# A perceiver block on one core: in 43 of the search's 64 steps the fourth tile's second count is made by ScalarE

## The reference, cut to what matters

```python
# channel_map: [16, 1601, 2048], x: [16, 64, 2048]
k = 38                                   # floor(0.6 * 64), made even
_, topk_idx = top_k(moveaxis(channel_map, 1, 2), k)      # 38 largest of 1601, for each of 16*2048 rows
mask = zeros((16, 2048, 64)).at[b, l, topk_idx].set(1.0) # only indices below 64 leave a mark
...                                      # two gated convolutions over mask * layernorm(x)
x = x + xattn(layernorm(x), channel_map, ...)
x = x + attention(layernorm(x), wq, wk, wv, wo)
x = x + ffn_with_experts(layernorm(x), ...)
```

## Time and profile before

| | |
|---|---|
| three runs | 2256.2, 2256.2, 2254.48 us |
| span of the profiled execution, first to last instruction | 2253.2 us (its own time is not listed apart) |
| the search, to the last decision of count a (L609 of step 64) | 651.1 us |
| TensorE busy | 1967.7 us, 87% |
| VectorE busy | 1368.3 us, 61% |
| ScalarE busy | 1062.3 us, 47% |
| GpSimd busy | 1185.0 us, 53% |

### The profile page before, as it was taken

How to read it: one execution, slowest core, us unless ns; L and a number is a source line. 1 busy time by engine, 2 the same in 40 slices (tenths; PEclk the granted TensorE clock), 3 DMA queues, 4 the chain that set the end, 5 groups by cost and what they waited for, 6 DMA issues and landing times. The chain is left out here.

```text
span 2253.2 us, 38992 instructions
## 1 busy us (share of the span) xinstructions
PE 1967.7 (87%) x14912; PEld 1573.5 (70%) x14912; DVE 1368.3 (61%) x2085; ACT 1062.3 (47%) x2441; POOL 1185.0 (53%) x1093
## 2 busy tenths in 40 slices
PE   4778788777761738999999999999999999999999
PEld 4666566555650237788778888877778878888887
DVE  6999999999999988744444611244446325631111
ACT  7877788788855665432332422232223322422222
POOL 3555555555546604755554546565555445644554
PEclk9999999999995869999999999999999999999999
DMA  9999999999942025522235443222254445434443
GB/s 388 376 369 373 329 327 326 310 314 325 335 150 80 17 68 163 173 81 78 82 109 178 141 138 115 88 77 81 80 173 141 127 145 192 146 117 136 139 137 114
DMA packets 158393, 407.67 MB, mean 181 GB/s; under 512 B 15616, under 2 KB 44544, under 8 KB 156544
## 3 DMA queue, kind: packets, MB, share of 16 engines
q1 hardware_dynamic: 157920, 403.55, 52.5%
q0 software_dynamic: 288, 1.64, 0.2%
HBM read 379.96 MB, written 25.17 MB: 180 GB/s over the span
## 5 line engine op out<-in xcount | busy, mean ns | idle before, releaser
L1348 POOL TENSOR_TENSOR t<-t,t 128x512 fp32r<-128x512 f32 (+1 forms) x488 | 650.0, 1343 | 662.8 <-ACT t L1341 590.9
L1899 PE MATMUL ps<-t,t 128*128 128x512 f32 x1856 | 739.0, 398 | 11.8 <-POOL t L1348 6.3
L1901 PE MATMUL ps<-t,t 128*128 128x512 f32 x1856 | 724.9, 391 | 0.0
L1900 PE MATMUL ps<-t,t 128*128 128x512 f32 x1856 | 724.5, 390 | 0.0
L1341 ACT ACTIVATE t<-t 128x512 fp32r<-128x512 f32 (+1 forms) x488 | 296.4, 608 | 697.0 <-PE ps L1901 372.8
L728 PE MATMUL ps<-t,t 128*128 128x128 bf16 (+1 forms) x6656 | 450.4, 222 | 165.0 <-DVE t L444 152.0
L728 PEld LDWEIGHTS ps<-t,t 128*128 128x128 bf16 x6656 | 388.9, 100 | 263.2 <-DVE t L444 231.0
L444 DVE TENSOR_SCALAR t<-t,t 128x1601 bf16<-128x1601 f32 x512 | 521.7, 1053 | 6.1 <-PE ps L728 2.0
L658 ACT ACTIVATE t<-t,t 128x1601 bf16<-128x1601 f32 x256 | 417.0, 1629 | 112.7 <-POOL t L686 110.3
L1899 PEld LDWEIGHTS ps<-t,t 128*128 128x128 f32 x1856 | 349.0, 188 | 92.2 <-POOL t L1348 11.0
L1901 PEld LDWEIGHTS ps<-t,t 128*128 128x128 f32 x1856 | 349.2, 188 | 74.7
(11 more groups left out here) (231 smaller groups left out, 1724.0 us busy)
## 6 DMA issues: line engine op xcount, KB each, us to landing
t<-ctxT SPq DMA_DIRECT2D x256, 800.5 KB, 6.5
t<-wqkv SPq DMA_DIRECT2D x192, 256.0 KB, 3.3
t<-wo SPq DMA_DIRECT2D x128, 256.0 KB, 4.7
t<-wb SPq DMA_DIRECT2D x128, 256.0 KB, 3.4
t<-xT SPq DMA_DIRECT2D x48, 256.0 KB, 6.6
t<-x1d SPq DMA_DIRECT2D x32, 256.0 KB, 4.9
x2d<-t SPq DMA_DIRECT2D x32, 256.0 KB, 2.0
t<-x2d SPq DMA_DIRECT2D x8, 1024.0 KB, 7.2
```

The source lines that it names most:

```text
L1348: e.tensor_tensor(wlo[r][:, 0:nk, :], raw[r][:, 0:nk, :], wh[r][:, 0:nk, :].bitcast(F32), ALU.subtract).then_inc(w_lo, 1)
L1899: e.matmul(bank[:, :], wh[r][:, q, :], xl, start=(kt == 0), stop=False)
L1900: e.matmul(bank[:, :], wlo[r][:, q, :], xh, start=False, stop=False)
L1901: m = e.matmul(bank[:, :], wh[r][:, q, :], xh, start=False, stop=(c == NCH[p] - 1 and q == nk - 1))
```

## The change

ScalarE makes count b of a quad's fourth tile, as a sum of signs, in 43 quads: g = 1 to 23, the odd g from 25 to 55, and 56 to 59. Quad g's count b falls into step g+1, so these are steps 2 to 24, the even steps 26 to 56, and steps 57 to 60. VectorE makes seven masks there. GpSimd makes the negated bound (`bound_b_gpsimd`) and takes the decision (`decide_b_gpsimd`). The order of the masks becomes b and c by turns. Where the quad two steps back is one of the 43, one b mask stands ahead of the decision of count b, otherwise two. GpSimd copies the candidates of two tiles in one instruction. The flags of the first 15 batches get five more operations. Some semaphores are merged, and an unused column block of the constants is left out.

```diff
+def by_act(g):
+    return 1 <= g < NQ - 4 and not (25 <= g + 1 <= 56 and g % 2 == 0)
+def front(i):
+    return 1 if by_act(i - 2) else 2
 def masks_of(i):
-    return [(k, u) for k, u in ORDER if (1 <= i <= NQ if k == "b" else 2 <= i <= NQ + 1)]
+    b = [("b", u) for u in range(3 if by_act(i - 1) else 4)] if 1 <= i <= NQ else []
+    c = [("c", u) for u in range(4)] if 2 <= i <= NQ + 1 else []
+    out = b[:front(i)]
+    b = b[front(i):]
+    while b and c:
+        out += [c.pop(0), b.pop(0)]
+    return out + b + c
...
     def sign_scalar(e, i, u):
...
+        if u == 2 and by_act(i - 1):
+            e.wait_ge(b_signed, ACT_NO[i - 1] + 1)
...
+    def sign_b_scalar(e, g):
+        n = 4 * g + 3
+        e.wait_ge(b_bound, ACT_NO[g] + 1)
+        e.wait_ge(signed, 4 * g + 6)
+        e.activation(scr[:, :], ring[n % NR][:, :], ACT.Sign, bias=nTB[:, g:g + 1], scale=SHRINK,
+                     accum_out=cntB[:, g % 8:g % 8 + 1]).then_inc(b_signed, 1)
...
     def search_scalar(e):
...
                 if u == 0 and 2 <= i:
                     counts_scalar(e, i - 1, 3)
+                if u == 1 and by_act(i - 1):
+                    sign_b_scalar(e, i - 1)
...
     def search_vector(e):
...
-                for u in range(2):
+                for u in range(front(i)):
                     mask_vector(e, i, "b", u, vg[:, u, 1:2])
...
-                e.wait_ge(counts_out, slot_of(i - 1, 3) + 1)
-                e.tensor_scalar(insB[:, 4 * c:4 * c + 4], sums[:, 4 * c:4 * c + 4], HIGH * K, None, ALU.is_lt).then_inc(b_dec, 1)
+                n = 3 if by_act(c) else 4
+                e.wait_ge(counts_out, slot_of(i - 1, n - 1) + 1)
+                e.tensor_scalar(insB[:, 4 * c:4 * c + n], sums[:, 4 * c:4 * c + n], HIGH * K, None, ALU.is_lt).then_inc(b_dec, 1)
                 e.wait_ge(b_dec, c + 1)
+                if by_act(c):
+                    e.wait_ge(b3_dec, ACT_NO[c] + 1)
...
+    def bound_b_gpsimd(e, g):
+        b, t = tile_of(4 * g + 3)
+        e.wait_ge(a_set, g + 1)
+        e.tensor_scalar(nTB[:, g:g + 1], v8[:, b % 2, t, 1:2], TINY, -1.0, ALU.max, ALU.mult).then_inc(b_bound, 1)
+
+    def decide_b_gpsimd(e, g):
+        e.wait_ge(b_signed, ACT_NO[g] + 1)
+        e.tensor_scalar(insB[:, 4 * g + 3:4 * g + 4], cntB[:, g % 8:g % 8 + 1], 2.0 * K - CM - 1.0, None,
+                        ALU.is_lt).then_inc(b3_dec, 1)
...
     def search_gpsimd(e):
...
+        for i in range(NQ):
+            if by_act(i - 2):
+                decide_b_gpsimd(e, i - 2)
+            bounds_gpsimd(e, i, 0)
+            if by_act(i - 1):
+                bound_b_gpsimd(e, i - 1)
+            copy_gpsimd(e, 4 * i)
+            if i >= 6 and (i - 6) % 4 == 0:
+                fin_gpsimd(e, (i - 6) // 4)
+            bounds_gpsimd(e, i, 1)
+            copy_gpsimd(e, 4 * i + 2)
+            quad_gpsimd(e, i)
```

More of the change, by code:

```diff
@@ L145 @@
 NQ = B * NT // 4
-ORDER = [("b", 0), ("b", 1), ("c", 0), ("b", 2), ("c", 1), ("b", 3), ("c", 2), ("c", 3)]
-def masks_of(i):
-    return [(k, u) for k, u in ORDER if (1 <= i <= NQ if k == "b" else 2 <= i <= NQ + 1)]
+def by_act(g):
+    return 1 <= g < NQ - 4 and not (25 <= g + 1 <= 56 and g % 2 == 0)
+ACT_B = [g for g in range(NQ) if by_act(g)]
+ACT_NO = {g: k for k, g in enumerate(ACT_B)}
+def front(i):
+    return 1 if by_act(i - 2) else 2
+def masks_of(i):
+    b = [("b", u) for u in range(3 if by_act(i - 1) else 4)] if 1 <= i <= NQ else []
[5 more added lines that the diff above has]
+    return out + b + c
 MASK_NO = {}
@@ L169, in slot_first @@
 def slot_first(i, u):
-    return MASK_NO[(i, "b", u)] if i <= NQ else MASK_NO[(i, "c", u)]
+    return min(MASK_NO[(i, k, u)] for k in "bc" if (i, k, u) in MASK_NO)
 def slot_last(i, u):
-    return MASK_NO[(i, "c", u)] if i >= 2 else MASK_NO[(i, "b", u)]
-def b_of(n):
-    return MASK_NO[(n // 4 + 1, "b", n % 4)]
+    return max(MASK_NO[(i, k, u)] for k in "bc" if (i, k, u) in MASK_NO)
 def c_of(n):
@@ L225, in build @@
     RS = (CM * 4 + 31) // 32 * 32
-    ring = [at(64 * KB + i * RS, [CM]) for i in range(NR)]
+    couples = [at(64 * KB + 2 * i * RS, [2, RS // 4]) for i in range(NR // 2)]
+    ring = [couples[i // 2][:, i % 2, 0:CM] for i in range(NR)]
+    heads = [couples[i][:, :, 0:C] for i in range(NR // 2)]
     o = 64 * KB + NR * RS
@@ L316, in build @@
     w16 = sb([16])
+    nTB = sb([NQ])
+    cntB = sb([8])
     sc = sb([80])
@@ L409, in setup_vector @@
     def setup_vector(e):
+        e.memset(nTB[:, :], -1.0)
         e.memset(fl2[:, :], 0.0).then_inc(set_up, 1)
@@ L485, in flags_vector @@
         w, wu = lsq[:, r], lsq[:, r].bitcast(U32)
+        nb, f3, ins3 = nTB[:, 4 * b0:4 * b1], last_of_four(f), last_of_four(insB[:, r])
+        w3, wu3 = w[:, 0:4 * (b1 - b0)], wu[:, 0:4 * (b1 - b0)]
         e.wait_ge(ln0_sqsum, 2 * NT)
-        for s in range(NFL):
+        for s in range(NFL[k]):
             if k or s:
-                e.wait_ge(flag_step, NFL * k + s)
+                e.wait_ge(flag_step, NFL[0] * k + s)
             if s == 0:
@@ L505, in flags_vector @@
                 i = e.tensor_tensor(f, f, w, ALU.max)
+            if s == 8:
+                i = e.scalar_tensor_tensor(w3, nb, -TINY, ins3, ALU.is_ge, ALU.mult)
+            if s == 9:
+                i = e.tensor_tensor(f3, f3, w3, ALU.max)
+            if s == 10:
+                i = e.tensor_scalar(wu3, nb.bitcast(U32), 0x7FFFFF, None, ALU.bitwise_and)
+            if s == 11:
+                i = e.tensor_scalar(w3, wu3, float(0x7FFFFF), None, ALU.is_equal)
+            if s == 12:
+                i = e.tensor_tensor(f3, f3, w3, ALU.max)
             i.then_inc(flag_step, 1)
@@ L638, in search_vector @@
                 maxima(1, 0)
-            for k, (kind, u) in enumerate(masks_of(i)):
-                if kind == "b" and u < 2:
+            todo = masks_of(i)
+            first = front(i) if i <= NQ else 0
+            for k, (kind, u) in enumerate(todo):
+                if k < first:
                     continue
                 mask_vector(e, i, kind, u, vg[:, u, 1:2] if kind == "b" else vc[:, u, 0:1])
-                done += 1
-                if 2 <= i < NQ and done == 3:
+                if 2 <= i < NQ and k == 2:
                     maxima(i, 1)
-                if 1 <= i < NQ - 1 and done == (4 if i == 1 else 7):
+                if 1 <= i < NQ - 1 and k == len(todo) - (1 if i == 1 else 2):
                     maxima(i + 1, 0)
-                if first_steps and i <= NQ + 1 and done <= 7:
-                    end_batch([done - 1])
+                if first_steps and k - first < 5:
+                    end_batch([2 + k - first])
                 if k == 4:
@@ L704, in quad_gpsimd, with copy_gpsimd @@
         e.tensor_tensor(eqb[y][:, four, :], v8[:, y, four, 0:7], v8[:, y, four, 1:8], ALU.subtract).then_inc(tied, 1)
-    def search_gpsimd(e):
[L707 to L718, removed]
+    def bound_b_gpsimd(e, g):
[6 more added lines that the diff above has]
+                        ALU.is_lt).then_inc(b3_dec, 1)
+    def copy_gpsimd(e, n):
+        b, t = tile_of(n)
+        if b >= 2 and t == 0:
+            e.wait_ge(fin, NF * (b - 2) + 8)
+        landed(e, n)
+        landed(e, n + 1)
+        e.tensor_copy(cand[b % 2][:, t:t + 2, :], heads[n % NR // 2]).then_inc(cand_copied, 1)
+    def search_gpsimd(e):
+        for i in range(NQ):
[10 more added lines that the diff above has]
+            quad_gpsimd(e, i)
     def count_tensor(e, i, kind, u):
@@ L784, in search_tensor @@
                     ln0_tensor(e, i, todo.pop(0))
+            for u in todo:
+                ln0_tensor(e, i, u)
     flags_max, flags_read, flags_all, row_in, turn_rows = (sem("flags_max"), sem("flags_read"), sem("flags_all"),
                                                            sem("row_in"), sem("turn_rows"))
-    turn_pick, turn_last, picked = sem("turn_pick"), sem("turn_last"), sem("picked")
+    turn_pick, turn_last, row_stage = sem("turn_pick"), sem("turn_last"), sem("row_stage")
+    PICKED, LEFT_KNOWN, OPENED = 1, 2, 3
     d_row, d_first = sem("d_row"), sem("d_first")
-    opened, segment, calm = sem("opened"), sem("segment"), sem("calm")
-    any_in, any_sum, flags_pool = sem("any_in"), sem("any_sum"), sem("flags_pool")
+    segment, calm = sem("segment"), sem("calm")
+    any_sum, flags_pool = sem("any_sum"), sem("flags_pool")
     any_left = ps[4][:, 0:1]
@@ L811, in first_pick_vector @@
         flags_vector(e, 0, 0, B - 1)
-        e.wait_ge(flag_step, NFL)
-        e.wait_ge(d_rid, 16)
+        e.wait_ge(flag_step, NFL[0])
+        e.wait_ge(d_const, N_CONST + 16)
         do = in_turn(e, turn_pick)
@@ L909, in rows_vector @@
             e.sem_inc(flags_max, 1)
-        e.memset(sm[:, 12:13], 0.0).then_inc(opened, 1)
+        e.memset(sm[:, 12:13], 0.0).then_inc(row_stage, 1)
     def gather_gpsimd(e, k, signal):
         e.wait_ge(masked, c_of(G_TILE[k]) + 1)
-        e.wait_ge(cand_copied, G_TILE[k] + 1)
```

(1 more changed line is left out.)

33 lines of the change are left out of this document (17 added, 16 removed).

## The result

The change makes the kernel slower, by a quarter of a per cent. Twenty runs gave a median of 2260.0 us (2254.6 to 2263.4) against 2254.4 us for twenty of the kernel before (2250.1 to 2259.9). The ratio is 1.0025, with a 95% interval of 1.0018 to 1.0032. I had forecast 2243.0 and a range up to 2254, a gain of 13.2 us where the medians show a loss of 5.6. The profiled execution has a span of 2260.4 us, 7.2 more than before.

A forecast was written before the change was run, and what follows sets the result against it. VectorE's order, mostly masks, was taken to bound the search, with ScalarE and the DMA close behind. Terms -1.7 - 13.8 + 1.2 + 1.1 = -13.2 us took the median from 2256.2 to 2243.0, range 2234 to 2254.

The forecast's parts named there:

- ScalarE's chain: ScalarE's distances from start to start in a step with the fifth sign: 9.64 us, or 9.97 with a square.
- A: Steps 2 to 24, 23 changed steps: 226.35 us before, forecast 224.7, a gain of 1.7 us.
- The rival in which ScalarE isn't the bound: Signs follow each other at 1.61 us, not 1.81; the DMA then sets steps 2 to 24; total 2229 us; 7%.
- The rival in which the DMA decides A: Steps 2 to 24: queues give only 364 GB/s, 9.97 us a step; total 2247.7 us; 12%.
- The bound's time: GpSimd's bound that sign 2 waits for: early by 0.5 us in ordinary steps, late by 0.6 with L472.
- B: Steps 26 to 56, 16 changed steps: VectorE stays the bound, 15.4 us go, 1.6 charged back, gain 13.8.
- The rival "B gives nothing": Steps 26 to 56: VectorE waits for ScalarE's fourth sign in each changed step; total 2255.8 us, no difference; 10%.
- C: Steps 57 to 60, 4 changed steps: 38.46 us before, forecast 39.7 by ScalarE's work, a loss of 1.2 us.
- Step 64: Five more flag operations over 60 elements, 0.22 us each, all on VectorE's path: 1.1 us more.
- The slower rival: TensorE's clock drops with less work; a whole low-level step costs up to 3.6 us, seven give 2268 us; 9%.

The follow-up runs named there:

- the run that should have lifted the clock alone: The changed kernel with 13 matmuls that nobody reads added in each of the 43 steps; 2261.9 us, ratio 1.0033 to the kernel before.

## Why the prediction was wrong

**ScalarE's chain: right.** I had 9.64 us a step, and the steps that nothing disturbs take 9.71. Over A that is 1.6 us. The rival in which ScalarE isn't the bound is gone: from sign 1 over the fifth sign to sign 2 it is 3.64 us in undisturbed steps, twice 1.82. The estimate of 1.52 us from sign to sign, worked out from figures of the Trainium skill (ScalarE: Activation LUTs, What ACT_TABLE_LOAD costs), is not what such a chain shows. The rival in which the DMA decides A did not come true either: 1.9 us of waits, and 377 GB/s in the run with VectorE's bounds. But it stands close behind: with two masks ahead VectorE waited 11.6 us in A for landings. The 358 GB/s of the Trainium skill (DMA: Bandwidth & Descriptors, Where 436 GB/s comes from) is no bound for this core's loads.

**The bound's time: the step that failed.** I took it that "the bound is early by 0.5 us in an ordinary step and late by 0.6 in a step with L472", with GpSimd's piece at 0.94 us "beside a mask". The 128 bounds before were all 1.09 us or less, so I never gave that number an upper end of its own. The change moves a mask from ahead of the decision of count b to between it and MAX8, and in that order 19 bounds take a mask's length more. Steps 6, 10, 14, 18 and 22 of A took 10.27 to 10.33 us instead of 9.71, 2.9 in all where I had nothing. The five steps with L494 took 4.7 over the chain where I had 3.0. The other 13 steps were 1.3 over. Together with the chain's 1.6 that is A's 7.6 us above the forecast. Steps 7 and 19, with L494 but without a long bound, were over the chain by 0.3 and 0.4, the three with a long one by 1.25 to 1.36, so the 0.6 that I had put on such a step was enough but for the long bounds. With two masks ahead, A was 227.4.

**B: 13.8 forecast, 5.1 measured.** The steps that are 2 modulo 4 gave what VectorE's mask promises: 81.9 us instead of 89.3, 7.4 less for eight masks. The steps with L494 have no fifth sign and I had let them be. Six of the eight grew from 10.31 to about 11.0 through a long bound and two to 10.39, 4.3 us in all. The changed steps behind them gave 3.2 instead of 7.7. Where ScalarE began late they took 10.0 us and more, its own chain with a square (9.97 in my sum), while VectorE alone would have come to about 9.5 (10.49 - 0.96); adding up pairs of steps had hidden that. The steps that are 1 modulo 4, which I hadn't counted, grew by 1.3, 0.6 of it by the long bound of step 49. The rival "B gives nothing" had the right place, ScalarE entering even steps late, but not the cause, and it took not all of the forecast gain but 8.7 of 13.8 us. I also miscounted the row: it held 30 steps. The gain is counted per mask, so this did not move the sum, but VectorE's pair of steps had 20.7 us and not 20.0.

**C: 1.2 forecast, 4.1 measured.** Long bounds in steps 58 and 59, and a clock of 0.84 with up to 1.5 us of waiting for TensorE. With two masks ahead the clock of C was 1.00 and C took 39.5, 0.2 from my figure. With the batch mask late it took 39.9 at a clock of 0.83, so the low clock by itself isn't what makes C long.

**Step 64.** The five flag operations stand in the timeline from 661.89 to 663.24, 1.35 us against 1.1.

```profile
661.89 0.26 DVE L531 SCALAR_TENSOR_TENSOR t<-t,t 128x60 f32<-128x60 f32 x1
...
662.94 0.26 DVE L539 TENSOR_TENSOR t<-t,t 128x60 f32<-128x60 f32 x1
663.24 0.41 DVE L885 TENSOR_TENSOR t<-t,t 128x240 f32<-128x240 f32 x1
```

**The slower rival.** TensorE's clock did fall, to 0.90 in A and 0.84 in C, as the rival had it. It isn't what made A slower: in the changed kernel's A VectorE never waits for TensorE and ScalarE once, for 0.5 us, where it waited 6.6 us in 12 times before. With the bounds on VectorE or with two masks ahead A fell to 224.7 and 227.4, but its clock rose to 0.94 too, so these two runs alone don't separate the causes, and the run that should have lifted the clock alone didn't lift it. The clock isn't harmless, though: it cost some 2.8 us of A with the batch mask late and part of C here.

**What stays open.** Why GpSimd's piece ends behind the second mask in one order and behind the first in the other. Steps 31 and 35 have the same instructions on VectorE at distances equal within 0.02 us, and differ. Shown is that the order with one mask ahead has such bounds (19 in the changed kernel, 8 with the fifth sign in B alone, none there once the batch mask stands late) and that the order with two has none.

## What to carry to other kernels

When work moves off the engine that binds, write down the receiving engine's whole chain for one step, and give every hand-over in it an upper bound: here a piece of two elements by a third engine was worth 0.9 us a time. Move work only where the receiver's chain has room: the same edit gained in B and lost in A. If a gain stays away, look for what stands ahead of the hand-over; a 1.2 us piece whose place was worth nothing without the fifth sign (ratio 1.0005 once moved) kept back 7 us of B with it. And sum the two chains step by step, not over pairs of unlike steps: a step of 9.5 us on one engine doesn't hide one of 10.0 on the other.

## What the runs showed of the hardware

GpSimd's bounds beside VectorE's masks end in steps of a mask. They take 0.22 us with VectorE idle, 0.94 to 1.11 beside masks, and 1.87 to 2.05 when they end one mask later. In steps 2 to 63 of the changed kernel the short ones for tiles 2 and 3 end 0.07 to 0.14 us behind the end of the first mask, the 19 long ones 0.04 us behind that of the second.

A sign that waits for the sum of the sign before it starts 1.82 us after it, and a pair of 512-column sums in float32 on TensorE takes 2.06 us at the lower level and 1.10 at full clock. TensorE's granted clock in A went from 0.96 to 0.90 when seven of eight masks were left to count, and 13 matmuls more per step (2418 in A, against 2411 before the change) left it at 0.89. With two masks ahead it was 0.94 with as few matmuls (2117). So the number of matmuls alone doesn't tell the clock.
